# Causal attention: the masks of scores and probabilities as half-array products on TensorE

## What is computed

```python
scores = jnp.einsum('bhqd,bhkd->bhqk', Q, K) / scale
causal = jnp.triu(jnp.ones((Tq, Tk), bool), k=1)
scores = jnp.where(causal[None, None], -jnp.inf, scores)
attn = jax.nn.softmax(scores, axis=-1)
out = jnp.einsum('bhqk,bhkd->bhqd', attn, V)
```

## Time and profile before

| | us |
|---|---|
| median of 3 runs (892.91 to 895.14) | 894.95 |
| the profiled execution | 895.08 |
| its span, first to last instruction | 893.3 |
| TensorE busy | 670.4 (75%) |
| VectorE busy | 483.9 (54%) |
| ScalarE busy | 385.5 (43%) |
| GpSimd busy | 347.6 (39%) |

### The profile page before, as it was taken

The page is one execution under the profiler, slowest core; times in us unless marked ns, Lnnn a source line. Parts: engine busy times, 40 slices in busy tenths (PEclk is TensorE's granted clock), DMA queues, the critical chain, the costliest instruction groups (busy, mean ns, idle before and its releaser), DMA issues. The chain is left out here.

```text
span 893.3 us, 21719 instructions
## 1 busy us (share of the span) xinstructions
PE 670.4 (75%) x7687; PEld 458.0 (51%) x7717; DVE 483.9 (54%) x1275; ACT 385.5 (43%) x948; POOL 347.6 (39%) x506
## 2 busy tenths in 40 slices
PE   1566648898996898994499999998406999999910
PEld 1343326676774454541155666665304877787700
DVE  1687446676772677773356888887341222222213
ACT  0344325575774012121056666667303665666500
POOL 4354240010011134342034477778841544455410
PEclk9988677899998899997589999999556999999965
DMA  3459831464302999999014333300111222212027
GB/s 95 132 152 182 209 114 24 80 108 81 74 3 38 208 239 209 216 219 228 7 23 77 72 90 87 84 26 26 43 36 48 59 55 61 58 55 64 28 72 222
DMA packets 93273, 87.17 MB, mean 98 GB/s; under 512 B 7785, under 2 KB 87921, under 8 KB 90097
## 3 DMA queue, kind: packets, MB, share of 16 engines
q1 hardware_dynamic: 84592, 74.70, 38.9%
q0 software_dynamic: 4352, 8.99, 3.2%
q10 hardware_dynamic: 4224, 2.10, 0.8%
HBM read 43.99 MB, written 41.76 MB: 96 GB/s over the span
## 5 line engine op out<-in xcount | busy, mean ns | idle before, releaser
L861 DVE TENSOR_REDUCE nm<-bank 128x8 f32<-128x1024 f32 x128 | 156.5, 1223 | 63.8 <-PE bank L633 61.7
L763 ACT ACTIVATE pr<-bank 128x512 f32<-128x512 f32 x256 | 147.2, 604 | 85.0 <-PE bank L657 82.2
L1572 DVE TENSOR_TENSOR exac<-bank,exsi 128x352 f32<-128x352 f32 x72 | 37.8, 525 | 127.8 <-PE bank L1479 121.0
L1029 POOL TENSOR_SCALAR_AFFINE_SELECT pr<-pr 128x1024 f32<-128x1024 f32 x64 | 69.7, 1088 | 75.3 <-ACT pr L763 75.1
L1451 POOL DMA_INDIRECT results<-exy,exre x72 | 70.8, 983 | 33.0 <-issue 33.0
L670 PE MATMUL bank<-pr,values 128*9 128x128 f32 x2048 | 82.3, 280 | 1.7 <-POOL pr L1029 1.7
L654 PE MATMUL bank<-qq,kk 48*128 48x128 bf16 x1024 | 76.8, 223 | 6.4 <-issue 4.2
L1308 PE MATMUL bank<-e0ch,expert_w 128*128 128x512 f32 x128 | 71.9, 644 | 8.2 <-DVE e0ch L1220 8.1
L657 PE MATMUL bank<-mt,pick 64*128 64x128 bf16 x1024 | 76.8, 223 | 0.0
L633 PE MATMUL bank<-kk,qq 48*128 48x128 bf16 x1024 | 55.5, 233 | 19.5 <-DVE nm L861 8.0
L1058 POOL DMA_INDIRECT sorted_in<-rrrow,rrpli x64 | 63.2, 988 | 14.2 <-issue 14.0
(11 more groups left out here) (203 smaller groups left out, 1304.3 us busy)
## 6 DMA issues: line engine op xcount, KB each, us to landing
sorted_in<-padding SPq DMA_DIRECT2D x8, 2145.0 KB
k_parts<-pj_parts SPq DMA_DIRECT2D x16, 384.0 KB, 2.9
kk<-k_parts SPq DMA_DIRECT2D x32, 192.0 KB
qq<-q_parts SPq DMA_DIRECT2D x32, 192.0 KB
exx<-sorted_in SPq DMA_DIRECT2D x72, 65.0 KB
kk<-k_parts SPq DMA_DIRECT2D x32, 128.0 KB
qq<-q_parts SPq DMA_DIRECT2D x32, 128.0 KB
coy<-results SPq DMA_DIRECT2D x8, 512.0 KB, 4.7
```

Of the source, the lines that this page charges most:

```text
L763: act.activation(probs[c], st_bank[(n * NC + c) % ST][:], ACT.Exp, scale=scale).then_inc(exp_s, 1)
L861: dve.tensor_reduce(neg_max[n % 2][:, u * 2 * C4:(u + 1) * 2 * C4], s_pair.rearrange("q (h k) -> q h k", k=T), AX_X, ALU.max, negate=True) ...
L1029: pool.affine_select(out=probs_pair[u][:], in_=probs_pair[u][:], compare_op=ALU.is_ge, fill=0.0, base=0, pattern=[[0, 2 * C4], [1, T]], ch ...
```

## The change

Both kinds of scores are masked by TensorE before the exponential, and GpSimd masks nothing. A mask is now made of half-array products: `future_h` and `later_h` hold the mask and its transpose as [contracted half, 128], once in rows 0 to 63 and once in rows 64 to 127, and `ident4h` four identities of 64 columns in both halves of the rows. `hide` writes the two banks of a pair with four products of 256 columns: two turns (64 of the 128 contracted rows each), in each turn one product per bank, in different halves of the array. `mix` waits for the exponentials alone.

```diff
+                    def hide(pair, of):
+                        for turn in range(2):
+                            for a in range(2):
+                                to = pair[a].rearrange("p (j c) -> p j c", c=T)
+                                pe.matmul(to[:, :, half(turn, HALF)], of[half(a, HALF), turn, :], ident4h[half(a, HALF), :, :],
+                                          start=turn == 0, stop=False, skip_group_check=True)
...
                         if causal:
-                            for a in range(2):
-                                pe.matmul(s_pair[:, a * 512:(a + 1) * 512], future[:],
-                                          ident4[:].rearrange("p a b -> p (a b)"), start=True, stop=False,
-                                          skip_group_check=True)
+                            hide([s_pair[:, a * 512:(a + 1) * 512] for a in range(2)], future_h)
...
                         pe.wait_ge(exp_s, earlier(k + 2 - ST))
                         to = [st_bank[(k + a) % ST] for a in range(2)]
+                        if causal:
+                            hide(to, later_h)
...
-                        if causal:
-                            pe.wait_ge(masked_s, n * PAIRS + c // 2 + 1)
-                        else:
-                            pe.wait_ge(exp_s, n * NC + c + 1)
+                        pe.wait_ge(exp_s, n * NC + c + 1)
...
-                    def mask(n, u):
-                        pool.wait_ge(exp_s, n * NC + 2 * u + 2)
-                        pool.affine_select(out=probs_pair[u][:], in_=probs_pair[u][:], compare_op=ALU.is_ge, fill=0.0, base=0,
-                                           pattern=[[0, 2 * C4], [1, T]], channel_multiplier=-1).then_inc(masked_s, 1)
...
-                        if causal and seq(n):
-                            mask(n, 0)
...
-                        if causal and seq(n):
-                            mask(n, 1)
```

The transposed products (L654) then add to what is there (`start=not causal`). In start-up GpSimd clears and fills one more matrix, `later`, and SyncE, after the last weight load, copies the halves by ten small DMAs and waits for them; the stage ends behind that:

```diff
                     sp.wait_ge(loaded, 16 * len(loads))
+                    sp.wait_ge(made, 5)
+                    for a in range(2):
+                        to = slice(a * HALF, (a + 1) * HALF)
+                        for k in range(2):
+                            of = slice(k * HALF, (k + 1) * HALF)
+                            sp.dma_start(future_h[to, k, :], future[of, :]).then_inc(halved, 16)
+                            sp.dma_start(later_h[to, k, :], later[of, :]).then_inc(halved, 16)
+                        sp.dma_start(ident4h[to, :, :], ident4[0:HALF, :, 0:HALF]).then_inc(halved, 16)
+                    sp.wait_ge(halved, 160)
```

More of the change, by code:

```diff
@@ L170, in build @@
         ident4 = sb("ident4", [128, 4, 128], BF16)
-        future = sb("future", [128, 128], BF16)
+        future, later = sb("future", [128, 128], BF16), sb("later", [128, 128], BF16)
+        ident4h = sb("ident4h", [128, 4, HALF], BF16)
+        future_h = sb("future_h", [128, 2, 128], BF16)
+        later_h = sb("later_h", [128, 2, 128], BF16)
         earlier_tokens = sb("earlier_tokens", [128, 128], BF16)
@@ L225, in prepare @@
             turned, kept, made, counted = sem("p_turned"), sem("p_kept"), sem("p_made"), sem("p_counted")
-            picked = sem("p_picked")
+            picked, halved = sem("p_picked"), sem("p_halved")
             with ExitStack() as own, nc.Block() as block:
@@ L254, in _ @@
                     pool.memset(future[:], 0.0).then_inc(zeroed, 1)
+                    pool.memset(later[:], 0.0).then_inc(zeroed, 1)
                     pool.memset(pick[:], 0.0).then_inc(zeroed, 1)
@@ L266, in _ @@
                     pool.memset(padding[:], 0.0).then_inc(zeroed, 1)
-                    pool.wait_ge(zeroed, 6)
+                    pool.wait_ge(zeroed, 7)
                     pool.iota(padding[:, :, ROW - 1:ROW].bitcast(I32), pattern=[[1, 1], [1, 1]], base=SPARE,
@@ L276, in _ @@
                                        pattern=[[1, 128]], channel_multiplier=-1).then_inc(made, 1)
+                    pool.affine_select(out=later[:], in_=later[:], compare_op=ALU.is_ge, fill=NEG, base=0,
+                                       pattern=[[-1, 128]], channel_multiplier=1).then_inc(made, 1)
                     pool.affine_select(out=earlier_tokens[:], in_=earlier_tokens[:], compare_op=ALU.is_gt, fill=0.0,
@@ L546, in attention @@
             s_ps, max_s, hi_s, split_s, mt_ps, mt_s = s("s_ps"), s("max"), s("hi"), s("split"), s("mt_ps"), s("mt")
-            st_ps, exp_s, masked_s, pv_s = s("st_ps"), s("exp"), s("masked"), s("pv")
+            st_ps, exp_s, pv_s = s("st_ps"), s("exp"), s("pv")
             ot_s, ot_ps, rec_s, norm_s, on_ps, on_s = s("ot"), s("ot_ps"), s("rec"), s("norm"), s("on_ps"), s("on")
@@ L557, in attention @@
                 max_t = [sb(f"mt{l}{p}", [128, T], BF16, own) for p in range(3)]
-                probs_pair = [sb(f"pr{l}{u}", [128, 2 * C4 * T], to=own) for u in range(PAIRS)]
-                probs = [probs_pair[c // 2][:, c % 2 * C4 * T:(c % 2 + 1) * C4 * T] for c in range(NC)]
+                probs = [sb(f"pr{l}{c}", [128, C4 * T], to=own) for c in range(NC)]
                 o_t = [sb(f"ot{l}{p}", [128, C4 * T], to=own) for p in range(2)]
@@ L654, in scores_t @@
                                 pe.matmul(to[a][:, j * T:(j + 1) * T], kk[buf][half(a, PROD), u * C4 + j, t],
-                                          qq[buf][half(a, PROD), u * C4 + j, t], start=True, stop=False, skip_group_check=True)
+                                          qq[buf][half(a, PROD), u * C4 + j, t], start=not causal, stop=False, skip_group_check=True)
                             for a in range(2):
@@ L762, in exponential @@
                         act.wait_ge(pv_s, earlier((n - 1) * NC + c + 1))
-                        act.activation(probs[c], st_bank[(n * NC + c) % ST][:], ACT.Exp, scale=scale).then_inc(exp_s, 1)
+                        act.activation(probs[c][:], st_bank[(n * NC + c) % ST][:], ACT.Exp, scale=scale).then_inc(exp_s, 1)
                     def keep_output(n):
```

## The result

The changed kernel takes 941.74 us (median of 5 runs, 939.22 to 949.95) beside 894.8 for the kernel before: ratio 1.055, interval 1.051 to 1.059. The forecast was 885.5, range 880 to 897. It is slower by 47 us, beyond the worst rival (905.5), and no rival names the cause. In all that follows a ratio is to the kernel before, run beside it on the same chip, with its 95% interval; the kernel before took 892 to 901 us there, so times of different versions are compared by their ratios.

What follows compares the result with a forecast made beforehand. It took the order of one step to count, TensorE running almost without pause beside an exponential loop with 0.19 us slack. Gains 0.4 + 5.3 + 3.0 + 3.0 - 2.0 = 9.7 us gave 885.5 us, range 880 to 897.

Steps and rivals of the forecast that it cites:

- the worst rival: Mask products of the second attention: halves don't overlap or weights load late, 20 us slower, 905.5 us; chance 0.10.
- (4): Routing part of the second attention: a batch of four steps takes 22.36 us, not 23.41; five batches gain 5.3 us.
- The last sentence of the forecast: Signs of being wrong: hides of 0.3 us or more, 2 us weight-load holes, or VectorE still stretched by indirect DMAs.
- (1): Score masks of the second attention: four half-array products take 0.22 us instead of 0.53; 0.10 of that is the array-mode change.
- (2): Transposed masks, new: four half-array products, 0.22 us, before each transposed group and inside the exponential loop.
- (3): Plain step of the second attention: 5.19 us, a gain of 0.06, bound by the exponential loop; seven steps gain 0.4 us.
- (5): Second attention's start at clock 0.50: seven pairs save 3.8 us, transposed hides give back 0.8; gain 3.0 us.
- (6) End: End of the second attention: of VectorE's 3.68 us wait behind GpSimd's queue of masks and indirect DMAs, 3.0 comes back.
- (7): Start-up stage: ten DMAs wait for the last load, nine more issues at 0.5 us each; cost 2.0 us (1 to 3).
- Rival (a): Mask products: halves don't overlap or weights load late, 0.63 us more for 32 steps, 905.5 us; chance 0.10.
- Rival (b): Code arrives late with 24 more instructions per step: one to three holes cost 2.3 to 7 us, 888 to 895; chance 0.12.

Runs made afterwards that it cites:

- two waits: The changed kernel, with GpSimd's two waits per step for the exponentials kept where its masks stood: 899.95 us, ratio 1.0087 to the kernel before.
- the changed kernel with bare waits: The changed kernel with GpSimd waiting for the exponentials, nothing else in front of its indirect DMAs: two waits a step 899.95 us, one wait 894.0.
- The best two versions that pace: The changed kernel with one GpSimd wait a step before both indirect DMAs, 894.0 us; with two waits, each followed by a mask-sized selection, 895.77.
- the version with two waits: The changed kernel with two GpSimd waits a step, a mask-sized selection on an unread tile after each: 895.77 us, ratio 1.0029 to the kernel before.
- a selection in front of each: The changed kernel without waits, with a mask-sized GpSimd selection on an unread tile before each indirect DMA: 923.11 us, ratio 1.0319 to the kernel before.

## Why the prediction was wrong

The step that failed is a cost that it put at nothing without a reason: in the sum for the batch (4), 22.36 us for each of five, GpSimd's indirect DMAs lose the masks between them and nothing follows from it. Measured are 31.4 to 34.3 us for each of the four batches with a burst (in the first of the five the burst begins only 3 us before the end). Under "the end" it takes the masks out of GpSimd's queue as a gain, and nowhere asks what then holds the indirect DMAs apart. Their waits are for the first of a batch only (placed, weighed, laid, tagged); the other seven had none but the mask ahead of them. The last sentence of the forecast looked for harm from indirect DMAs, but to VectorE.

By its own numbers:

- (1) Score masks: right. 0.22 in the place of 0.53; alone they give 0.49 per plain step. The 0.10 that it put down to the change from whole to half array is gone with the full products, but no run takes it apart from the columns.
- (2), (3) Transposed masks and plain step: right. 5.20 for 5.19, the hide waits for the exponential (25 waits of L636 for L781, 6.3 us). The 0.49 of one part is given back as 0.44 by the other. So in plain steps the whole change gains a tenth of what its first half gains alone.
- (4) Batch: right for what it priced. 6.11, 5.91, 5.30, 5.20 are 22.52 against 22.36, and VectorE isn't stretched. This shows only in the batch before the first indirect DMAs. With them a batch takes 31.4 to 34.3 us in a burst and 25 to 26 with two waits. This is the 48.8 us.
- (5) Start: a pair takes 2.36 as forecast; the gain is 2.2 and not 3.0.
- (6) End: wrong. The wait of 3.68 us did shrink to 0.7, but from the last step's transpose to the last indirect DMA it is 28.8 us before, 29.8 after and 28.9 to 29.0 in the changed kernel with bare waits. The wait was not what set the end; the term of 3.0 is nothing.
- (7) Start-up: 2.6 (18.30 to 20.90) for 2.0; each DMA took 0.64 to issue and not 0.5.
- Rival (a) is out, the halves overlap. Rival (b), code that arrives late, most likely came true beside the rest: all eight kernels with both kinds of half-array products have one hole of 3.1 to 4.8 us in front of the mixture's weights in the same step, and that step takes 9.3 to 11.9 us and not 5.2; none of the seven others has it there. In each of the eight traces a packet of 16 KB on the queue of instructions lies inside the hole and ends 1.4 to 1.6 us before it does (478.13 to 479.53 for the hole that ends at 481.13). That fits late code, but no run varied it. The rival has a chance of 0.12 in the forecast and costs 4 to 6.6 us.

With the hole (6), without the gain at the end (3) and with the smaller terms (1.4), the forecast would have been 896. The best two versions that pace came to 894.0 and 895.8, but that closeness is partly luck: their batches with indirect DMAs take 25.4 and 24.3 us and not 22.4, 9 to 12 us in all, and the second attention begins 2.3 and 6.3 us sooner in their traces than before, in spite of the longer start-up. A part of that, 2.6 and 3.5 us, lies in the first attention, which no version touches: it took 164.6 to 168.4 us in the eight traces with both kinds of half-array products, with one hole of 3.0 to 5.3 us in front of weight loads, and 168.2 to 169.8 in the seven others, with two or three that add up to 4.6 to 7.4. Why the holes move is not shown. The burst adds some 45 us to either sum.

Of the Trainium skill, SBUF — State Buffer, section Who interferes with whom, the part on VectorE holds here (0.19 us with the masks gone, 0.80 under them). The same section says that TensorE and ScalarE never wait on anyone. Here a signal from TensorE to ScalarE takes 8.2 us beside a burst, and TensorE pauses for 0.44 us and the like inside it; as a rule on SBUF's ports it may stand, but it doesn't cover what indirect DMAs of GpSimd do, and the measurement decides.

## What to carry to other kernels

Before work is taken from an engine, look at what else stands in its queue and ask what held that back; a wait that looks like a cost may be the brake of the instructions behind it. Here two waits that keep the brake are worth 42 us. And time each half of a change alone: the masks of the scores gain 0.8% without the rest in one comparison and 0.35% in another, the transposed ones spend it.

## What was unexpected of the hardware

- While GpSimd issues indirect DMAs back to back beside the steps of the attention, signals of TensorE to ScalarE and VectorE arrive late: 8.2 us for eight that follow about every 1.3 us, up to 2.1 after the start of the first of two, 0.6 or 1.3 to 1.6 after the start for a single one. A gap of 0.4 us with an iota in it let one through, and ScalarE's signal to TensorE passed in 0.05.
- The last sixteen indirect DMAs of the stage follow each other as closely in all versions but one, and hold no signal in any of the fifteen traces (0.04 us at most). Nor is a single one always a hindrance: behind a selection of 1.09 us 25 of 26 signals were free in the kernel before and 23 of 30 in the version with two waits, but 17 of 26 with the score masks in halves and 4 of 16 with a selection in front of each; behind a tiny product of 0.19, 10 of 53. Why is open. Fewer rows or shorter indirect DMAs were not tried.
- A hole of 3 to 5 us in front of a weight load, once, in the same step of every kernel with both kinds of half-array products, which ends 1.4 to 1.6 us after a packet of instructions has landed.
